# Degrees and graph convolution in one stage of two sweeps, moments of the next norm in its finish, feed-forward norm by two VectorE operations per block

## What is computed

```python
def _layernorm(x, axis=-1, eps=1e-5):
    m = jnp.mean(x, axis=axis, keepdims=True)
    v = jnp.var(x, axis=axis, keepdims=True)
    return (x - m) / jnp.sqrt(v + eps)

def _L0_gnn_ref(x, adj, W, b):
    D = jnp.sum(adj, axis=1)
    d_inv_sqrt = jnp.power(D + 1e-09, -0.5)
    adj_norm = adj * d_inv_sqrt[:, None] * d_inv_sqrt[None, :]
    h = adj_norm @ x
    out = h @ W.T + b
    return jax.nn.relu(out)

# in _L1_ffn_ref, with d = 64 per head
    hn = layernorm(mixed + resid, ln_g, ln_b)
    fx = f_n.reshape(b, s, nh, d)
    pm = fx == 0
    hx = jnp.where(pm, 0.0, fx @ fc1_w.T + fc1_b)
    hx = jax.nn.relu(hx)
    hx = jnp.where(pm, 0.0, hx @ fc2_w.T + fc2_b)
    hx = layernorm(hx + fx, fnorm_g, fnorm_b)
    fout = hx.reshape(b, s, h)
    fg = jax.nn.softmax(fout @ fgate_w.T, axis=-1)
    return (fout.reshape(b, s, nh, d) * fg[..., None]).reshape(b, s, h)

# the two layers
    x = x + _L0_gnn_ref(_layernorm(x), adj, ...)
    x = x + _L0_ffn_ref(_layernorm(x)[None], ...)
    x = x + _L1_gnn_ref(_layernorm(x), adj, ...)
    x = x + _L1_ffn_ref(_layernorm(x)[None], ...)
```

## Time and profile before

| | us |
|---|---|
| median of 3 runs (lowest, highest) | 3788.89 (3787.19, 3790.59) |
| the profiled execution, its own time | 3786.82 |
| its span, first to last instruction | 3785.1 |

### The profile page before, as it was taken

One profiled execution on the slowest core, in us unless ns is written; L12 is line 12 of the kernel. 1 busy time (PEld: TensorE's weight loads), 2 busy tenths in 40 slices (PEclk: granted clock), 3 DMA queues, 4 the chain that ended last, 5 costly groups with the idle time before them and its releaser, 6 DMA issues. The chain is left out here.

```text
span 3785.1 us, 46076 instructions
## 1 busy us (share of the span) xinstructions
PE 3116.6 (82%) x18162; PEld 1886.5 (50%) x18162; DVE 1725.4 (46%) x2736; ACT 1263.9 (33%) x1715; POOL 1858.7 (49%) x992
## 2 busy tenths in 40 slices
PE   0499955567599978899999999978999999999944
PEld 0144533345478855555555555545555555555422
DVE  5200143333777344555656555215565555564025
ACT  2100011101455312333443444423334443444445
POOL 0000000011333202567787888964677888889924
PEclk9999978868799987999999999979999999999967
DMA  8754100010899700000000000000000000000001
GB/s 346 290 145 139 59 5 0 2 48 7 252 274 280 134 19 1 1 1 1 1 1 1 1 1 1 1 1 1 1 1 1 1 1 1 1 1 1 1 4 36
DMA packets 74117, 195.37 MB, mean 52 GB/s; under 512 B 8627, under 2 KB 25521, under 8 KB 67250
## 3 DMA queue, kind: packets, MB, share of 16 engines
q1 hardware_dynamic: 49154, 148.11, 10.8%
q0 software_dynamic: 24752, 44.31, 6.5%
HBM read 188.99 MB, written 3.41 MB: 51 GB/s over the span
## 5 line engine op out<-in xcount | busy, mean ns | idle before, releaser
L1807 POOL TENSOR_TENSOR at_acc<-at_acc,at_pt 128x1024 f32<-128x1024 f32 (+3 forms) x728 | 1556.9, 2139 | 278.3 <-ACT at_pt L1643 195.2
L1703 DVE TENSOR_REDUCE at_mx<-at_psR 128x2 f32<-128x1024 f32 (+3 forms) x784 | 859.1, 1113 | 855.8 <-PE at_psR L1534 540.0
L1643 ACT ACTIVATE at_pt<-at_psR 128x1024 f32<-128x1024 f32 (+3 forms) x784 | 731.5, 936 | 993.6 <-PE at_psR L1555 603.5
L1571 PE MATMUL at_psO<-at_pt,v 128*64 128x512 f32 (+3 forms) x3136 | 707.5, 572 | 16.3 <-DVE at_oT L1722 10.6
L303 PE MATMUL gcn_acc<-gcn_ring,xn 128*128 128x512 f32 (+1 forms) x728 | 293.2, 565 | 149.4 <-DMA gcn_ring<-in_adjT 149.2
L1552 PE MATMUL at_psR<-at_qhi,at_klo 64*128 64x512 f32 (+3 forms) x1568 | 345.9, 435 | 59.1 <-ACT at_pt L1643 28.0
L1534 PE MATMUL at_psR<-at_khi,at_qhi 64*128 64x512 f32 (+3 forms) x1568 | 341.0, 429 | 34.7 <-ACT at_pt L1643 10.3
L1571 PEld LDWEIGHTS at_psO<-at_pt,v 128*64 128x64 f32 x3136 | 194.2, 139 | 339.4 <-issue 275.7
L1187 PE MATMUL ga_acc<-h,ga_ring 128*128 128x257 f32 (+1 forms) x1352 | 304.4, 386 | 31.1 <-ACT ga_ring L1091 26.1
L1552 PEld LDWEIGHTS at_psR<-at_qhi,at_klo 64*128 64x128 f32 x1568 | 151.9, 187 | 331.4 <-issue 307.7
L1552 PE MATMUL at_psR<-at_qlo,at_khi 64*128 64x512 f32 (+3 forms) x1568 | 300.4, 376 | 0.0
(11 more groups left out here) (305 smaller groups left out, 3109.3 us busy)
## 6 DMA issues: line engine op xcount, KB each, us to landing
deg_rows<-in_adj SPq DMA_DIRECT2D x26, 1664.0 KB, 13.8
ga_rows<-in_adj SPq DMA_DIRECT2D x26, 1664.0 KB, 9.7
gcn_ring<-in_adjT SPq DMA_DIRECT2D x78, 512.0 KB, 3.7
ga_ring<-in_adjT POOLq DMA_DIRECT2D x78, 512.0 KB, 23.9
gcn_ring<-in_adjT SPq DMA_DIRECT2D x13, 256.0 KB, 2.7
ga_ring<-in_adjT POOLq DMA_DIRECT2D x13, 256.0 KB, 9.8
X<-in_x SPq DMA_DIRECT2D x1, 3200.0 KB
out_x<-X SPq DMA_DIRECT2D x6, 512.0 KB
```

Source lines behind the costliest of these rows:

```text
L1571: ins = pe.matmul(psO[lanes[l], off:off + w], v1[:, t, (2 * hp + l) * D:(2 * hp + l + 1) * D], pt[:, g % PTS, l, 0:w], start=g == FIRST[u] ...
L1643: act.activation(pt[:, g % PTS, :, 0:w], psR[:, slot_of["score", g] % SLOTS, :, 0:w], ACT.Exp).then_inc(e_ready, 1)
L1703: dve.tensor_reduce(mx[:, u % 2, :, s, c:c + 1].rearrange("p l o -> p (l o)"), psR[:, slot_of["max", i] % SLOTS, :, 0:w], AX.X, ALU.max).t ...
L1807: pool.tensor_tensor(to, to, got, ALU.add).then_inc(added, 1)
```

## The change

The two first stages become one (`stage_gcn` with x_in and adj), in two sweeps over the k tiles.

- First sweep: eight accumulator banks hold four blocks (`SWEEP` = 2048 columns) at a time. For each token tile t SP loads the row tile of adj (3 buffers) and 128 x 2048 of adjT (4 buffers), VectorE and ScalarE sum the row tile, and the tile's norm and its degree are taken together: root of (variance + eps) * degree on ScalarE, its reciprocal, one `tensor_scalar` that writes `xs[:, t, :]`. TensorE multiplies tile t into all four blocks, eight matmuls of 512 columns.
- Second sweep: blocks 4, 5 and the tail with the old ring of 13 pairs, its first 13 loads queued behind those of the first sweep. After each pair from the third on, one tile's projection, ten in each block (four in the tail), into the two halves of what was block 3's accumulator; the last two tiles follow at the end.
- The finish takes a `bn_stats` and a `bn_aggr` of each finished tile into `mv1`, which lives on to the next stage; `LayerNorm` gets it as `mv` and leaves out its own.
- In the feed-forward stage `norm(b)` goes from ScalarE (16 operations of 64 elements) to VectorE (two of 1024: less the mean, times the reciprocal of the deviation); `shift1` goes. norm(0) and norm(1) stand ahead of the loop, norm(b + 2) behind `mask_hidden(b)`.

The core of the diff:

```diff
@@ class LayerNorm, vector
+        if not self.moments_known:
             for t in range(NT):
                 ins = eng.bn_stats(self.stats[:, t, :], self.X[:, t, :])
...
@@ stage_gcn, new: queue of SP
+                def load_rows(t):
+                    if t >= ROWS:
+                        sp.wait_ge(sum_v, t - ROWS + 1)
+                        sp.wait_ge(sum_a, t - ROWS + 1)
+                    sp.dma_start(rows[:, t % ROWS, :], adj[t * P:(t + 1) * P, :]).then_inc(rows_loaded[t % ROWS], 16)
+                def load_cols(t):
+                    if t >= COLS:
+                        sp.wait_ge(cols_used, t - COLS + 1)
+                    sp.dma_start(cols[:, t % COLS, :], adjT[t * P:(t + 1) * P, 0:SWEEP]).then_inc(cols_loaded[t % COLS], 16)
...
+                for n, k, i in TURN:
+                    c0, w = LATE[n]
+                    if n:
+                        sp.wait_ge(late_used, i - PAIRS + 1)
+                    sp.dma_start(ring[:, k, :, 0:w], src[:, k, :, c0:c0 + w]).then_inc(late_loaded[k], 16)
@@ TensorE
+                for t in range(NT):
+                    pe.wait_ge(cols_loaded[t % COLS], (t // COLS + 1) * 16)
+                    pe.wait_ge(xs_ready, t + 1)
+                    order = [(c, b) for c in range(DC) for b in range(4)]
+                    if t == NT - 1:
+                        order = [(c, b) for b in range(4) for c in range(DC)]
+                    for c, b in order:
+                        ins = pe.matmul(acc[:, b, c, :], xs[:, t, c * P:(c + 1) * P], cols[:, t % COLS, b * BLK:(b + 1) * BLK],
+                                        start=(t == 0), stop=(t == NT - 1))
...
+                        if k >= 2 and turned < min(EARLY_TILES + SUB * n, 10 * (n + 1)):
+                            project()
@@ VectorE, first sweep
+                for t in range(NT):
+                    dve.wait_ge(rows_loaded[t % ROWS], (t // ROWS + 1) * 16)
+                    dve.reduce_sum(part[:, 0, t:t + 1], rows[:, t % ROWS, 0:SPLIT], AX.X).then_inc(sum_v, 1)
...
+                    dve.scalar_tensor_tensor(vd[:, t:t + 1], mv[:, t, 1:2], LN_EPS, deg[:, t:t + 1], ALU.add,
+                                             ALU.mult).then_inc(vd_ready, 1)
+                    if t + 1 < NT:
+                        statistics(t + 1)
+                    dve.wait_ge(root_ready, t + 1)
+                    link(dve.reciprocal(scale[:, t:t + 1], root[:, t:t + 1]))
+                    dve.tensor_scalar(xs[:, t, :], X[:, t, :], mv[:, t, 0:1], scale[:, t:t + 1], ALU.subtract,
+                                      ALU.mult).then_inc(xs_ready, 1)
@@ stage_ffn, VectorE (the loop of 16 activations on ScalarE goes)
+                def norm(b):
+                    t0, ws = tiles(b)
+                    v = groups_of_block(b)
+                    mean = hn_mv[:, t0:t0 + ws, :, 0].rearrange("p t n -> p (t n)")
+                    link(dve.tensor_tensor(v, v, per_group(mean, b), ALU.subtract))
+                    dve.tensor_tensor(v, v, per_group(rstd1[:, t0 * NH:(t0 + ws) * NH], b), ALU.mult).then_inc(normed, 1)
...
+                norm(0)
+                norm(1)
                 for b in range(NBLK):
                     mask_hidden(b)
+                    if b + 2 < NBLK:
+                        norm(b + 2)
```

More of the change, by code:

```diff
@@ new lines, in statistics @@
+                def statistics(t):
+                    dve.wait_ge(x_loaded[[t < b for a, b in PIECES].index(True) if t < NT - 1 else 2],
+                                32 if t >= PIECES[2][0] else 16)
+                    link(dve.bn_stats(stats[:, t % 2, :], X[:, t, :]))
+                    link(dve.bn_aggr(mv[:, t, :], stats[:, t % 2, :]))
+                statistics(0)
+                for t in range(NT):
+                    dve.wait_ge(rows_loaded[t % ROWS], (t // ROWS + 1) * 16)
+                    dve.reduce_sum(part[:, 0, t:t + 1], rows[:, t % ROWS, 0:SPLIT], AX.X).then_inc(sum_v, 1)
+                    dve.wait_ge(sum_v, t + 1)
+                    dve.wait_ge(sum_a, t + 1)
+                    dve.scalar_tensor_tensor(deg[:, t:t + 1], part[:, 0, t:t + 1], 1e-9, part[:, 1, t:t + 1], ALU.add,
+                                             ALU.add).then_inc(deg_ready, 1)
+                    dve.wait_ge(deg_ready, t + 1)
+                    dve.scalar_tensor_tensor(vd[:, t:t + 1], mv[:, t, 1:2], LN_EPS, deg[:, t:t + 1], ALU.add,
[6 more added lines that the diff above has]
+                                      ALU.mult).then_inc(xs_ready, 1)
@@ L1989, in _ @@
             def _(act):
-                def norm(b):
-                    t0, ws = tiles(b)
-                    v = groups_of_block(b)
-                    for g in range(ws * NH):
-                        i = t0 * NH + g
-                        ins = act.activation(v[:, g, :], v[:, g, :], ACT.Identity, bias=shift1[:, i:i + 1],
-                                             scale=rstd1[:, i:i + 1])
-                    ins.then_inc(normed, 1)
                 def turned(b):
@@ L2060, in _ @@
                         gates(b - 1)
-                    if b + 2 < NBLK:
-                        norm(b + 2)
                 squares(NBLK - 1)
```

346 lines of the change are left out of this document (156 added, 190 removed).

## The result

The changed kernel takes 3642.2 us (median, 3640.5 to 3644.1); the kernel before took 3789.2 beside it. The ratio is 0.961, with a 95% interval from 0.960 to 0.962: 147 us less. The forecast was 3644. The profiled execution took 3640.5 us around a span of 3638.5, against 3785.1 before, so 146.6 us have to be found in the two traces. The mean granted clock was nearly the same (0.926 before, 0.924 after).

What follows compares the result with a forecast made beforehand. The first stage was taken as bound by DMA, the second by TensorE, neither using what the other waits for. Savings of 130.3 + 10.4 + 4 = 144.7 us from 3788.9 gave 3644 us, range 3634 to 3668.

Steps and rivals of the forecast that it cites:

- Part 1: Merged first stage: TensorE starts on the adjacency earlier, so the stage ends at 339.4 instead of 469.7, 130.3 us less.
- the loads' 6.40: First sweep: a tile's row and transpose loads take 6.40 us at 430 GB/s, less than TensorE's 6.89.
- The second sweep: Merged stage, remaining blocks and tail with 24 projections between the matmuls: from 200.2 to 334.0 us.
- The start: First tiles of the first sweep, bound by DMA: TensorE's waits about 14 us, tile 3 starting at 41.7 us.
- Part 2: Moments taken in the finish: the next stage no longer computes its own statistics on its chain, 10.4 us less.
- Part 3: Feed-forward norm moved from ScalarE to VectorE: 9 us gained at the start, 5 given back, 4 us less net.
- The three steps of the sum: Feed-forward start: norm(0) 4.3 us earlier, norm(1) 1.3 more, norm(2) 2.8 more, sum 8.4 us.
- Given back: Feed-forward blocks 4, 5 and 6, normed beside GpSimd's mix: 2.5 + 1.9 + 0.6, 5 us back, bounds 0 and 6.3.
- no meeting on SBUF: Rival, feed-forward: GpSimd has finished or the norm slips in between, part 3 gives its 9 us: 3639; chance 0.13.
- DMA as the bound of the first sweep: Rival: loads take 7.8 us per tile, 0.9 more than TensorE, 21 us on 23 tiles: 3665; chance 0.15.
- A whole sweep at 1.2 GHz: Rival: waits keep TensorE at its lower clock, 13.8 us per tile in the first sweep: 3816; chance 0.03.
- No row buffer and no accumulator slot held the sweep: Rival: an unsatisfied wait on a row buffer or accumulator slot costs 10 to 40 us: 3654 to 3684; chance 0.05.

Runs made afterwards that it cites:

- after_again: The changed kernel run once more without any edit, as the neighbour of other runs on its chip: 3642.6 us.
- norm_only: The kernel before with only the feed-forward norm moved from ScalarE to two VectorE operations: 3783.5 us, ratio 0.998.
- best: The changed kernel with X loaded in two-tile pieces, the norm of feed-forward blocks 4 to 6 on ScalarE, 127-row transfers split into 112 and 15: 3622.2 us.
- more_load: The changed kernel with 1.57 MB of loads that nobody reads added to each tile's 2.75 MB in the first sweep: 3731.2 us.

## Why the prediction was right

**Part 1, forecast 130.3, measured 125.8.** TensorE's 6.89 us per tile, the loads' 6.40 and so a sweep bound by TensorE: right. SyncE issued the row loads 6.48 us apart until 130 us and 6.87 apart after that, so the loads had 0.39 us of room per tile and used it to catch up. The second sweep was put at 133.8 us (200.2 to 334.0); from 205.3 to 339.0 (326.76 + 12.25 in the tail) it was 133.7. VectorE's 3.7 us from a landed row to scaled rows: 9.07 to 12.79 us. The start was the step that was mis-sized: tile 3 was put at 41.7 us and began at 47.0. The 14 us of waiting in that sum do not come out of its own landings (12.7, 23.5, 33.6 and 41.3 leave 7.8), but the 41.7 do. Measured was one wait, 9.1 us, where waits before tiles 1 to 3 had been forecast, and 4.3 us of slower matmuls beside it, where 1.9 at most had been allowed for: 2.9 in tiles 0 and 1 (16.63 us for 13.78, though the granted clock reads 1.00 there) and 1.4 in tile 2 (at 0.79). What the sum missed is that the last tile's 127 rows go through one DMA engine and hold the queue behind them. With them split, tile 2 began at 33.0 and the stage ended at 338.3, where 339.4 was forecast: what else was off in that step came to about 1 us in all. The sign was there to be read before: in the kernel before, too, the final store moved mostly 24 GB/s.

**Part 2, forecast 10.4, measured 10.2** in the full change and 10.1 when undone alone.

**Part 3, forecast 4 net, measured 9.0 in the first profile**, 6.9 in after_again's and 6.3 as a part alone. Both of its terms were off, to the same side.
- At the start 9 us were forecast. From the reciprocal to the first block's weighing it was 43.3 us before, and 11.8 less in the first profile, 10.3 in after_again, 9.3 in norm_only. The three steps of the sum, 8.4 us, are in all of them. It missed a fourth: the kernel before took 3.65 us for the first pass of the third block, behind waits of 2.05 us for a norm and of 1.90 us, and with the new norm it is 1.98 in every trace. This is the row before:

```profile
3678.45 3.65 PE L1950 MATMUL ff_psF<-ff_fxT,ff_fc 128*128 128x512 f32 x4 [1.90 <-ACT ff_fxT L2005]
```

What differs between the runs is the clock at which TensorE comes back in the second pass of the first block. In the kernel before it took 3.78 us behind 3.71 of waiting. With the new norm the wait is 2.46 us in every run, and behind it the pass took 1.98 in the first profile and in best, 2.78 in after_again and 3.78 in norm_only:

```profile
3519.11 2.78 PE L1978 MATMUL ff_psF<-ff_h1T,ff_fc 128*128 128x512 f32 x4 [2.46 <-DVE ff_h1T L2088]
3655.83 3.78 PE L1956 MATMUL ff_psF<-ff_h1T,ff_fc 128*128 128x512 f32 x4 [2.46 <-DVE ff_h1T L2066]
```

The granted clock over it was 1.00 in the first profile and 0.50 in norm_only. The other traces of the new norm lie between (2.45 to 3.47 us). So 2.5 us of this part come and go from one execution to the next, and the first profile's 9.0 had luck.

- Given back: forecast 5, measured 2.1 to 2.6 (75.7 to 76.1 us for the five periods, 73.5 before). The mechanism stood as forecast: two-input operations on VectorE and GpSimd's take turns, and each GpSimd operation that waits becomes 0.86 us longer (3.21 for 2.35; 0.33 beside the half block). I had charged the whole 1.23 us of each VectorE operation. By the profile's times GpSimd's second operation is issued at 3541.62, and VectorE's has been running since 3541.40 (its end less 1.22), so GpSimd would wait for the rest of it alone. Against an undisturbed period of 14.6 us the three blocks are 1.7, 1.8 and 0.7 longer, 4.2 in all, so the 5 were nearly right. The 2.1 come out because the first and the third period of the kernel before were longer already (15.48 and 15.81): in them TensorE's second pass took 2.53 and 2.84 us for 1.88.
- The rival "no meeting on SBUF" had the better number for this part in the first profile (9) and is false: they meet, in three blocks. The Trainium skill, "SBUF — State Buffer", section "SBUF: two separate sides", calls it an exclusive lock for a whole instruction; the ends that follow one another above, and 1.22 us without the mix, agree.
- The weights of the stage came 1.1 us later than before, seen from its first operation (8.78 us of waiting for 7.63), and took that much from the gain. The cause of this stays open.

**The sum.** 144.7 was forecast, 146.6 came in the traces and 147 in the medians. In the traces part 1 brought 4.5 us less than its forecast and part 3 brought 5.0 more, and 1.6 came from code that nothing changed. The near hit of the total is luck: the errors cancelled.

**The rivals.** DMA as the bound of the first sweep needs loads of more than 6.89 us per tile, and they took 6.48; more_load shows what such a sweep looks like. A whole sweep at 1.2 GHz did not come even there. No row buffer and no accumulator slot held the sweep: behind tile 2 it has no wait.

## What to carry to other kernels

A stage that is all loads and one that is all matmuls can be merged when a unit's bytes take less time than its matmuls (here 6.48 and 6.89 us); what remained of the first stage was the first unit's way in (12.9 us) and the waits of the start. Look at what the queue does in those first microseconds: here a single transfer of 127 rows cost 5.4 us there, and it showed as a sixteenth of the usual GB/s. An operation with two SBUF inputs put on VectorE beside GpSimd's made both wait here, so place it in blocks where GpSimd is idle. And before a gain of a few us is put down to an edit, read a second trace of the same kernel: TensorE's clock may have come back earlier or later in it.
